# A GNN block: the attention layers load their one-hot matrices from a record that the convolution stored, and VectorE scales all gathered rows

## What is computed

```
h = relu(layernorm(x));  x = x + conv(h)          # edge weights from a small MLP, products with the gathered source rows,
                                                  # segment sum over the destination, linear maps out
h = relu(layernorm(x));  x = x + gat(gat(h))      # two attention layers, 4 heads of 64 features:
z = h @ W;  el, er = (z * al).sum(-1), (z * ar).sum(-1)
e = leaky_relu(el[src] + er[dst], 0.2)
ex = exp(e - segment_max(e, dst)[dst]);  alpha = ex / segment_sum(ex, dst)[dst]
out = elu(segment_sum(z[src] * alpha, dst) + h + b)
```

## Time and profile before

| | |
|---|---|
| runs without the profiler | 3516.74, 3520.89, 3521.0 us |
| the profiled execution: span | 4581.9 us (nothing that lies around the span is given) |
| busy in it: TensorE / VectorE / ScalarE / POOL | 68% / 53% / 38% / 56% |
| mean granted TensorE clock | 0.611 of full speed; 0.75 from 300 to 1600 us (convolution), 0.53 from 1900 to 3100 us (layer 0) |
| DMA | 442.78 MB, 97 GB/s over the span |

### The profile page before, as it was taken

One profiled execution on the slowest core, in us unless ns is written; L12 is line 12 of the kernel. 1 busy time (PEld: TensorE's weight loads), 2 busy tenths in 40 slices (PEclk: granted clock), 3 DMA queues, 4 the chain that ended last, 5 costly groups with the idle time before them and its releaser, 6 DMA issues. The chain is left out here.

```text
span 4581.9 us, 78327 instructions
## 1 busy us (share of the span) xinstructions
PE 3134.4 (68%) x20204; PEld 1904.6 (42%) x20205; DVE 2415.9 (53%) x7011; ACT 1756.2 (38%) x6334; POOL 2565.8 (56%) x2634
## 2 busy tenths in 40 slices
PE   7677777667677777477767776776466667666666
PEld 5344444344444444244444444444244334433433
DVE  6444554444455445355555555555355555555555
ACT  6122211121222122355555554554345445554554
POOL 6554444444444443566666666663566666666663
PEclk8777777777777777555555555555555555555555
DMA  7222222222222222333333333332333333333332
GB/s 238 84 86 83 81 81 81 78 80 85 82 80 82 82 85 74 99 102 103 102 105 101 103 102 106 100 102 76 99 101 101 106 105 100 101 109 100 102 101 81
DMA packets 241741, 442.78 MB, mean 97 GB/s; under 512 B 83665, under 2 KB 134933, under 8 KB 241567
## 3 DMA queue, kind: packets, MB, share of 16 engines
q0 software_dynamic: 119808, 334.13, 26.7%
q1 hardware_dynamic: 121887, 108.14, 7.7%
HBM read 381.95 MB, written 60.10 MB: 96 GB/s over the span
## 5 line engine op out<-in xcount | busy, mean ns | idle before, releaser
L1673 POOL DMA_INDIRECT nodes<-z_rows,scratch x1664 | 1674.4, 1006 | 1048.6 <-issue 501.9
L1111 POOL DMA_INDIRECT scratch<-h_rows,scratch x832 | 817.1, 982 | 892.7 <-DVE nodes L1261 676.2
L1635 ACT ACTIVATE nodes<-nodes 128x64 f32<-128x64 f32 x3328 | 816.3, 333 | 6.2 <-issue 6.2
L1155 PE MATMUL ce_part<-nodes,scratch 128*32 128x128 f32 (+1 forms) x6656 | 459.4, 391 | 151.0 <-issue 133.9
L1748 PE MATMUL ge_part<-nodes,scratch 128*32 128x260 f32 x3328 | 449.9, 633 | 5.7 <-ACT nodes L1635 5.7
L1640 ACT COPY scratch<-ge_part 128x260 f32<-128x260 f32 x208 | 78.1, 375 | 958.2 <-issue 635.0
L1909 DVE TENSOR_TENSOR_SCAN scratch<-scratch,ge_runs 1x36 f32<-1x36 f32 x208 | 45.1, 217 | 755.3 <-remote 685.7
L1723 PE MATMUL ge_runs<-ident,scratch 1*36 1x1 f32 x832 | 76.4, 192 | 527.9 <-DVE scratch L1910 491.9
L1289 DVE TENSOR_TENSOR nodes<-nodes,ce_sum 128x512 f32 x105 | 72.3, 689 | 660.7 <-remote 389.9
L1155 PEld LDWEIGHTS ce_part<-nodes,scratch 128*32 128x32 f32 x6656 | 254.9, 139 | 360.3 <-issue 299.0
L1135 PE MATMUL ce_w<-fc_sb,scratch 64*128 64x256 f32 x1664 | 313.1, 507 | 107.6 <-ACT scratch L1030 95.4
(11 more groups left out here) (271 smaller groups left out, 5538.3 us busy)
## 6 DMA issues: line engine op xcount, KB each, us to landing
nodes<-z_rows,scratch POOLq DMA_INDIRECT x1664
nodes<-hT SPq DMA_DIRECT2D x56, 256.0 KB
scratch<-h_rows,scratch POOLq DMA_INDIRECT x832
z_rows<-scratch SPq DMA_DIRECT2D x28, 264.0 KB
z_rows<-nodes SPq DMA_DIRECT2D x28, 264.0 KB
hT<-scratch SPq DMA_DIRECT2D x28, 256.0 KB
hT<-nodes SPq DMA_DIRECT2D x28, 256.0 KB
nodes<-x_rows SPq DMA_DIRECT2D x28, 256.0 KB
```

The lines of the kernel that those rows point to most:

```text
L1111: nc.gpsimd.indirect_dma_start(xg[u][:, i * D:(i + 1) * D], None, m.h_rows, bass.IndirectOffsetOnAxis(ap=idx[r][:, k:k + 1], axis=0)).then ...
L1155: ins = nc.tensor.matmul(here, hots[u][:, at:at + TW], these, start=(q == 0 and c == 0), stop=(q == 1), skip_group_check=True)
L1635: ins = nc.scalar.activation(head_rows(r, k, h), head_rows(r, k, h), ACT.Copy, scale=zg[r][:, at:at + 1])
L1673: nc.gpsimd.indirect_dma_start(zg[r][:, k * ZW:(k + 1) * ZW], None, m.z_rows[layer], bass.IndirectOffsetOnAxis(ap=idx[r][:, k:k + 1], axis ...
```

## The change

A DRAM array `places` of one record per step, 128 partitions x 512 values (256 KB): selection matrix, one-hots, picks. The convolution computes all three into one of two record buffers and SP stores each record. The attention layers drop `one_hots`, `node_picks` and `stage_places`; SP loads the record of step v+3 into one of four buffers, once `window_sums` of step v-1 is done with that buffer, and TensorE waits for the record in `block_er`. ScalarE no longer scales rows: VectorE scales the even tiles of step v+1 where it did, and the odd tiles after `within_tiles`. The convolution's one-hots take the layers' order of tiles (odd and even apart), and its harmonics are copied in that order. The diff, cut:

```diff
@@ conv_stage @@
-        pick = nodes_part(NW, 2)
-        hot = nodes_part(G * TW, 1)[0]
+        rec = [nodes_part(PLACES, 1)[0], m.lin1[:, :, :].rearrange("p c n -> p (c n)")]
+        selT, hot, pick = [list(a) for a in zip(*[places_of(a) for a in rec])]
...
+            def store_places(v, u):
+                sp.wait_ge(pick_ready, v + 1)
+                sp.dma_start(places_row(m, v), rec[u]).then_inc(st_places[u], 16)
...
                     load_x(slot.n, quad)
+                store_places(v, r % 2)
                 if ahead >= 2:
                     sp.wait_ge(hid_ps, v + 2)
                     load(v + 2)
...
-            def one_hots(v, r):
+            def one_hots(v, r, stored):
+                u = r % 2
                 dve.wait_ge(staged_ready, v + 1)
-                relative_places(V, rel.rearrange("p (j t) -> p j t", j=NB), staged[r]).then_inc(rel_ready, 1)
+                if stored is not None:
+                    dve.wait_ge(st_places[u], stored)
+                V.tensor_tensor(rel.rearrange("p (q j) -> p j q", j=NB), tiles, beyond.broadcast_to([P, NB, 2]), ALU.subtract
+                                ).then_inc(rel_ready, 1)
+                V.tensor_tensor(selT[u].rearrange("p (j n) -> p j n", j=NB),
+                                m.drop[:, :].rearrange("p (o n) -> p o n", o=1).broadcast_to([P, NB, TW]),
+                                beyond.broadcast_to([P, NB, TW]), ALU.is_equal)
                 dve.wait_ge(rel_ready, v + 1)
-                one_hots_of(V, m, hot, rel).then_inc(hot_ready, 1)
+                V.tensor_tensor(hot[u].rearrange("p (k n) -> p k n", k=G), ...).then_inc(hot_ready, 1)
@@ gat_stage @@
+        rec = [scratch(PLACES) for r in range(4)]
+        selT, hot, pick = [list(a) for a in zip(*[places_of(a) for a in rec])]
...
+            def load_places(v, r):
+                sp.dma_start(rec[r], places_row(m, v)).then_inc(rec_in[r], 16)
...
+            for r in range(3):
+                load_places(r, r)
             for r in range(4):
                 load_er(r, r)
...
+                if ahead >= 3:
+                    sp.wait_ge(summed, v + 1)
+                    load_places(v + 3, (r + 3) % 4)
                 if ahead >= 4:
                     sp.wait_ge(er4_ps, v + 1)
                     load_er(v + 4, r)
...
-                act.wait_ge(ex_ready, v * 2 + 2)
-                for k in range(1, G, 2):
-                    for h in range(HEADS):
-                        at = k * ZW + D + h
-                        ins = nc.scalar.activation(head_rows(r, k, h), head_rows(r, k, h), ACT.Copy,
-                                                   scale=zg[r][:, at:at + 1])
-                ins.then_inc(rows_act_ready, 1)
                 act.wait_ge(part_summed, v + 5)
...
-                if ahead >= 4:
-                    act.wait_ge(pick_ready, v + 1)
-                    stage_places(nc, act, m, v + 4, group, staged[r], columns[r], staged_ready)
...
             def block_er(v, r, loaded):
-                pe.wait_ge(hot_ready, v + 1)
+                pe.wait_ge(rec_in[r], loaded)
                 pe.wait_ge(hotT_ready, v + 1)
                 pe.wait_ge(er_in[r], loaded)
-                nc.tensor.matmul(ps_er4, selT, erw[r], start=True, stop=True).then_inc(er4_ps, 1)
+                nc.tensor.matmul(ps_er4, selT[r], erw[r], start=True, stop=True).then_inc(er4_ps, 1)
...
                 if q == 0:
-                    pe.wait_ge(rows_scaled, v + 1)
                     pe.wait_ge(sums_ready, v + 1)
-                else:
-                    pe.wait_ge(rows_act_ready, v + 1)
+                pe.wait_ge(rows_scaled, v * 2 + (q + 1))
...
-            def scale_even_rows(v, r):
-                dve.wait_ge(ex_ready, v * 2 + 1)
-                scale_rows(r, 0, NB)
-                scale_rows(r, NB, G).then_inc(rows_scaled, 1)
+            def scale_half(v, r, q):
+                if q == 0:
+                    dve.wait_ge(ex_ready, v * 2 + 1)
+                scale_rows(r, q, NB + q)
+                scale_rows(r, NB + q, G).then_inc(rows_scaled, 1)
...
-                if ahead >= 3:
-                    one_hots(v + 3, (r + 3) % 4)
-                node_picks(v, r)
                 if ahead >= 1:
                     into_tiles(v + 1, 1 - u)
...
                     differences(v + 1, 1 - u)
-                    scale_even_rows(v + 1, (r + 1) % 4)
+                    scale_half(v + 1, (r + 1) % 4, 0)
                 if ahead >= 2:
                     within_tiles(v + 2, u, quad * 64 + ((r + 2) // 2 + 1) * 32)
+                if ahead >= 1:
+                    scale_half(v + 1, (r + 1) % 4, 1)
```

More of the change, by code:

```diff
@@ L56 @@
 ZW = D + 2 * HEADS
+PLACES = NB * TW + G * TW + NW
 LOW = -1.0e38
@@ L852, in stage_places, with places_of, places_row, one_hot @@
     nc.scalar.copy(columns, m.pick_cols[:, bass.ds(first, NW)]).then_inc(staged_ready, 1)
[L855 to L871, removed]
+def places_of(rec):
+    a, b = NB * TW, NB * TW + G * TW
+    return rec[:, 0:a], rec[:, a:b], rec[:, b:PLACES]
+def places_row(m, v):
+    return m.places[bass.ds(v, 1), :, :].rearrange("o p w -> (o p) w")
+def one_hot(hot, k):
+    at = ((k % 2) * NB + k // 2) * TW
+    return hot[:, at:at + TW]
 def conv_stage(nc, m):
@@ L941, in conv_stage @@
         ea8_in = sem("ea8_in")
+        st_places = [sem(f"st_places{u}") for u in range(2)]
         x_in, y_in, s_pX, s_x1, s_bn, s_mv, s_sd, s_rs, s_nm, s_h, s_pT, s_hT, s_pZ, s_rows, st_x1, st_hT, st_rows, dve_go = [
@@ L1000, in _ @@
             sp.sem_inc(s_h, 1)
-            for st in (st_x1, st_hT, st_rows):
+            for st in (st_x1, st_hT, st_rows, *st_places):
                 sp.sem_inc(st, 16)
@@ L1008, in _ @@
             sp.wait_ge(ea8_in, last_quad * 64 + 64).then_inc(sp_done, 1)
+            for st in st_places:
+                sp.wait_ge(st, last_quad * 32 + 48).then_inc(sp_done, 1)
             with sp.Fori(first, REAL, 2) as n:
@@ L1342, in step @@
                 if ahead >= 1:
-                    one_hots(v + 1, (r + 1) % 4)
+                    one_hots(v + 1, (r + 1) % 4, quad * 32 + (r + 1) // 2 * 16 + 16)
                 if r == 2:
@@ L1414, in gat_stage @@
         zg = [part(G * ZW) for r in range(4)]
-        hot = [scratch(G * TW) for r in range(4)]
+        rec = [scratch(PLACES) for r in range(4)]
+        selT, hot, pick = [list(a) for a in zip(*[places_of(a) for a in rec])]
         hotT = scratch(2 * P)
-        selT = scratch(NB * TW)
-        pick = [scratch(NW) for u in range(2)]
-        columns = [scratch(NW) for r in range(4)]
-        staged = [scratch(STAGED) for r in range(4)]
-        rel = scratch(G)
         idx = [scratch(G).bitcast(I32) for r in range(4)]
@@ L1609, in last_rows @@
                 nc.scalar.copy(b.rows[:, t * ZW:(t + 1) * ZW], b.tables[t][:, 0:ZW]).then_inc(s_rows, 1)
-            groups = [stage_sources(nc, act, m, r, idx[r], idx_ready) for r in range(4)]
             for r in range(4):
-                stage_places(nc, act, m, r, groups[r], staged[r], columns[r], staged_ready)
+                stage_sources(nc, act, m, r, idx[r], idx_ready)
             for v in range(2):
@@ L1751, in tile_sums, with window_sums @@
                 return ins
-            def window_sums(v, u):
+            def window_sums(v, r):
+                u = r % 2
                 pe.wait_ge(sums_ready, v + 2)
-                pe.wait_ge(pick_ready, v + 1)
                 for c in range(2):
-                    nc.tensor.matmul(ps_sum[u][:, c * NW:(c + 1) * NW], sums[:, c * P:(c + 1) * P], pick[u],
+                    nc.tensor.matmul(ps_sum[u][:, c * NW:(c + 1) * NW], sums[:, c * P:(c + 1) * P], pick[r],
                                      start=False, stop=True, skip_group_check=True)
-                nc.tensor.matmul(ps_sum[u][0:HEADS, 2 * NW:3 * NW], sums[:, D:D + HEADS], pick[u],
+                nc.tensor.matmul(ps_sum[u][0:HEADS, 2 * NW:3 * NW], sums[:, D:D + HEADS], pick[r],
                                  start=False, stop=True, skip_group_check=True).then_inc(summed, 1)
@@ L1839, in step @@
                 factors(v, u)
-                window_sums(v, u)
+                window_sums(v, r)
             all_steps(pe, last_quad, step)
@@ L2018, in _ @@
             differences(0, 0)
-            one_hots(2, 2)
             scores(1, 1, 16 * G)
             place_er(2)
-            scale_even_rows(0, 0)
+            scale_half(0, 0, 0)
             within_tiles(1, 1, 32)
+            scale_half(0, 0, 1)
             slot = Mem()
```

54 lines of the change are left out of this document (22 added, 32 removed).

## The result

The changed kernel takes 3535.03 us (median of five runs, 3526.72 to 3546.53), the kernel before 3519.97 (five runs). The ratio is 1.0048, 95% interval 1.0030 to 1.0065: some 15 us slower, less than half a per cent. The forecast was 3550.

What follows compares the result with a forecast made beforehand. The prediction took POOL's back-to-back gathers to bound the kernel; to the base of 3521 us it added 29 us for longer gathers in the layers and 0 for the rest, giving 3550 us, range 3440 to 3640.

Steps and rivals of the forecast that it cites:

- The stalls are the profile's alone, and POOL sets the pace: All stages: VectorE's 1075.6 us of unexplained waits belong to the profiled execution only; the runs take what POOL's gathers need.
- the sum of 3505: Kernel before: 3240 us for all 2496 gathers with their gaps plus 265 us outside them, 0.4% under the median.
- the hand-over sets the pace: Rival, layers: VectorE, TensorE and ScalarE's hand-over bounds the kernel and the change shortens it, 3436 us; chance 0.21.
- ScalarE's scalings are worth nothing, VectorE's 0.48 us per step are hidden: Layers: dropping ScalarE's 16 scalings gains 0; VectorE's added 0.48 us per step hides behind 10.45 us of gathers.
- The cover's size of 1.5 us: Layers: the hand-over, 8.95 us a step, fits under POOL's 10.45 with 1.5 us to spare.
- VectorE lengthens the gathers in the layers: Layers: second scaling pair adds 1.19 us per quad to gathers, dropped one-hots take 0.64 off; +29 us over 52 quads.
- delays cancel: Rival, layers: the second scaling pair costs POOL what the one-hots did, so no change, 3521 us; chance 0.12.
- The Trainium skill's lock: Layers: VectorE and GpSimd share an exclusive port pair and the loser waits a whole instruction; up to 287 us.
- The convolution, 0: Convolution: added selT (271 ns) and a 256 KB store per step taken as 0; without cover 28 us.
- The convolution's gathers stay at 982: Convolution: sign of the forecast that the gathers' mean length remains 982 ns after the change.
- The record's wait is nearly hidden: Layers: block_er's new wait for the record load, 1.07 us late at r = 1, taken as 0.
- The record comes late: Rival, layers: the record lands 4.5 us after issue and delays the hand-over, +127 us, 3648 us; chance 0.12.

Runs made afterwards that it cites:

- second profile: The kernel before, unchanged, profiled once more: 3518.02 us, span 3516.2, without the stalls of the first profile.
- e1: The changed kernel, but ScalarE scales the odd tiles again, so records without VectorE's second pair of scalings: 3499.66 us.
- e7: The changed kernel, but SP issues a step's record load only after the hand-back of the same step: 3597.75 us.
- e2: The kernel before, but VectorE scales all eight tiles, the odd ones after the scans, without records: 3568.29 us.
- e3: The changed kernel with each 128x512 scaling on VectorE cut into two of 128x256: 3700.06 us.
- e4: The kernel before with only the convolution's half of the change, records made and stored but not loaded by the layers: 3535.0 us, ratio 1.0045.

## Why the prediction was right, and where not

*The stalls are the profile's alone, and POOL sets the pace*: right. The second profile has no stall, and the rest of the span is 988 to 995 us whatever the gathers do, where POOL doesn't wait. That the sum of 3505 came so near was helped by luck: in the second profile all gathers take 836.4 + 1685.7 = 2522 us, 31 more than in the stalled one, and what lies ahead of, between and behind the stages 234 us, 31 less than the prediction's 265. The rival "the hand-over sets the pace" (3436) is refuted: in e1 ScalarE keeps its 16 scalings, and POOL waits no longer than in the changed kernel.

*ScalarE's scalings are worth nothing, VectorE's 0.48 us per step are hidden*: right (rest 995 with ScalarE's 16 scalings, in e1, and 993 without). The cover's size of 1.5 us fits e7, where 1.9 us a step more of waiting in TensorE made POOL wait 0.2 us a step in layer 0 and less than 0.1 in layer 1; it was not measured by itself.

*VectorE lengthens the gathers in the layers*, +62 us for the second pair, -33 for the one-hots, +29 in sum: changed alone, each came out near its size (+59.5 in e2, -31.2 in e1), the sum did not. Together they make +9.9 in the profiles and by the medians nothing (15.1 us for the whole change, 16.7 for the convolution's part alone); after the records, the second pair adds only 41.1. That each size was met is in part luck: the prediction took one quad of layer 0 for all 52, but the one-hots' share lies in layer 0 alone, and two thirds of the second pair's in layer 1. The prediction added two losses that depend on where gathers and instructions meet, and each moves the other. The rival "delays cancel" was right here, by two thirds in the profiles and wholly by the medians. How the places shift in the layers wasn't followed further.

*The Trainium skill's lock* ("SBUF — State Buffer", section "SBUF: two separate sides"): the page says that whoever starts first gets the port pair for the whole instruction and that the other fully blocks. The prediction read it as a whole instruction lost each time, up to 287 us. e2 pays 59.5 / 416 = 0.14 us for each added instruction of 0.68, since a gather is held only if its start falls into one (or just before it, 0.09 us at 1703.22), and loses what is left of it. There the measurement decides against the prediction's reading; a block that lasts until the instruction ends agrees with it. That the gather of 1703.22, which started first, is held by the later scaling is not what the page says. And e3 shows 1.44 us lost to a run of instructions of 0.41, more than "the loser waits for the whole instruction" allows for one of them. The prediction's own quad had such a run: the gather of 2415.42 started 0.07 us before the first of the one-hot instructions, not inside one, and ended at 2417.01, 0.83 us after L864 (2416.18).

*The convolution, 0*: this is the term that was mis-sized, +20.0 us. The prediction weighed the store as a wait on SP and `selT` as time of VectorE; both are nearly free, as it said (some 3 us without the store). It didn't ask what 256 KB per step do to the landing of the gathers, and through that to the place of VectorE's longest instruction against POOL. "The convolution's gathers stay at 982" failed: 1029, against 1005 in the second profile of before.

*The record's wait is nearly hidden*: right, 66.6 us of waits and no trace of them in the rest. "The record comes late" (3648) didn't happen; with 1.9 us a step more of waiting in e7, it cost 63 us.

So 3550 came near 3535 by luck, through two errors of opposite sign. In the profiles the layers cost 19 us less than forecast and the convolution 20 more. By the medians the layers cost nothing of the 29 and the convolution 16.7 us; that difference and a base 1 us lower (3519.97 for 3521) make nearly all of the 15 us by which the forecast was off.

## What to carry to other kernels

Where one engine runs back to back, sum its instructions and look at the rest of the span: if the rest is constant from version to version, only what lengthens those instructions counts, and work that is moved beside them costs by where it meets them, not by its own length. Two such effects that were each measured alone need not add, so the pair has to be run. Traffic that nobody waits for can still move an engine that is timed by another transfer's landing.

## What the runs showed of the hardware

- An indirect gather on POOL that starts while VectorE runs a 128x512 or 128x1024 instruction with two SBUF inputs loses what is left of that instruction less 0.13 us (0.79 of 0.92 and 0.93 of 1.05 above). One that starts 0.09 us ahead of it can lose the same way (0.63 us at 1703.22). One that starts inside a product with an input in PSUM loses nothing (0.95 us at 701.48; in e4 none of the 119 that start inside L1267 loses over 0.02 us).
- VectorE instructions that close up behind each other can hold a gather for their whole run: 1.44 us for four of 0.41 in e3, where the layers' gathers have a mean of 1115 ns.
- The store of 256 KB a step, 27.3 MB in all, cost 13.5 us. It let the gathered rows land later (2.11 us after the gather's end in place of 1.92, medians) and did not make the gathers themselves slower: of the convolution's gathers those that meet the 128x1024 product lost 14.6 us more, all together 12.0.
